# Macaron layer: the first layer's two K halves joined in PSUM, and one native group in place of two

## What is computed

```
x = x + 0.5 * ffn(layernorm(x))
x = x + mixer(layernorm(x))
x = x + 0.5 * ffn(layernorm(x))

ffn(x):   h  = layernorm(x) * gamma + beta
          w1 = (fc1_q - 128) * fc1_scales        # 256 x 1024, one scale per 128 rows and column
          y  = silu(h @ w1 + fc1_bias)
          w2 = (fc2_q - 128) * fc2_scales        # 1024 x 256, one scale per 128 rows and column
          return x + 0.5 * (y @ w2 + fc2_bias)

mixer(x): a = sigmoid(x @ Wa + ba); b = x @ Wb + bb; c = tanh(x @ Wc + bc); d = x @ Wd + bd
          s_t = a_t * s_(t-1) + (1 - a_t) * b_t
          return (c * s) @ Wy + by + d
```

## Time and profile before

| | |
|---|---|
| median of 3 runs | 780.07 us (779.71 to 782.04) |
| the profiled execution | 778.86 us, its span 777.0 us |
| TensorE busy | 736.8 us (95%) |
| ScalarE busy | 663.8 us (85%) |
| VectorE busy | 640.0 us (82%) |
| GpSimd busy | 636.8 us (82%) |
| mean granted clock | 0.985 of 2.4 GHz |

### The profile page before, as it was taken

One profiled execution on the slowest core, in us unless ns is written; L12 is line 12 of the kernel. 1 busy time (PEld: TensorE's weight loads), 2 busy tenths in 40 slices (PEclk: granted clock), 3 DMA queues, 4 the chain that ended last, 5 costly groups with the idle time before them and its releaser, 6 DMA issues.

```text
span 777.0 us, 14017 instructions
## 1 busy us (share of the span) xinstructions
PE 736.8 (95%) x3262; PEld 549.8 (71%) x3262; DVE 640.0 (82%) x1242; ACT 663.8 (85%) x1123; POOL 636.8 (82%) x821
## 2 busy tenths in 40 slices
PE   5698999999999999999999996989999999999996
PEld 4366777777777776668788783667777777777774
DVE  5377989999999998878778864779899999999886
ACT  5877999999999998778888887779989999999984
POOL 6588999999999987848666676889999999999853
PEclk7989999999999999999999999899999999999999
DMA  8640000000000000000000000000000110000001
GB/s 258 194 135 1 2 0 0 0 0 0 0 0 0 2 0 1 1 1 0 0 0 0 1 1 1 0 29 28 28 27 27 34 48 27 27 27 28 28 28 56
DMA packets 19820, 20.24 MB, mean 26 GB/s; under 512 B 1548, under 2 KB 19394, under 8 KB 19778
## 3 DMA queue, kind: packets, MB, share of 16 engines
q1 hardware_dynamic: 19680, 19.74, 7.8%
q10 hardware_dynamic: 98, 0.02, 0.0%
HBM read 11.37 MB, written 8.39 MB: 25 GB/s over the span
## 4 chain that ended last, share of the span: by engine, by line
PE 84%; issue 5%; POOL 5%; ACT 2%; DVE 2%; DMA 1%; ACTq 0%; DVEq 0%; POOLq 0%
PE ps_fc L867 28%; PE ps_z L867 26%; PE ps_z L901 13%; PE ps_fc L967 7%; PE ps_tr L860 4%; PE ps_tr L917 3%; POOL h_lo L393 2%; PE ps_fc L975 2%; POOL g_lo L403 1%; PE ps_fc L961 1%; DVE z_acc L685 1%; PE ps_z L860 1%; DMA rows<-in_L_attn_bc 1%; POOL xhat L372 1%; ACT xhat L532 0%
## 5 line engine op out<-in xcount | busy, mean ns | idle before, releaser
L685 DVE SCALAR_TENSOR_TENSOR z_acc<-ps_z,cols,z_acc 128x512 f32<-128x512 f32 x384 | 276.7, 742 | 25.2 <-PE ps_z L867 23.7
L403 POOL TENSOR_TENSOR g_lo<-g_full,g_hi 128x512 fp32r<-128x512 f32 x192 | 248.5, 1295 | 49.9 <-ACT g_hi L569 47.5
L547 ACT ACTIVATE u_sb<-ps_fc,cols 128x512 f32<-128x512 f32 x256 | 199.6, 780 | 60.8 <-PE ps_fc L867 54.9
L867 PE MATMUL ps_fc<-h_hi,q_sb 128*128 128x512 f32 x512 | 227.0, 443 | 6.1 <-DVE y_sb L674 3.9
L674 DVE SCALAR_TENSOR_TENSOR y_sb<-ps_fc,cols,u_sb 128x512 f32<-128x512 f32 x256 | 190.3, 743 | 50.5 <-ACT u_sb L547 50.4
L867 PE MATMUL ps_fc<-h_lo,q_sb 128*128 128x512 f32 x512 | 202.9, 396 | 0.0
L867 PE MATMUL ps_z<-g_hi,q_sb 128*128 128x512 f32 x384 | 155.2, 404 | 12.0 <-DVE z_acc L685 11.9
L867 PE MATMUL ps_z<-g_lo,q_sb 128*128 128x512 f32 x384 | 152.3, 397 | 0.0
L567 ACT ACTIVATE g_full<-y_sb 128x512 f32<-128x512 f32 x192 | 120.0, 625 | 9.8 <-DVE y_sb L674 9.8
L867 PEld LDWEIGHTS ps_fc<-h_hi,q_sb 128*128 128x128 f32 x512 | 97.7, 191 | 33.4 <-DVE y_sb L674 7.1
L901 PE MATMUL ps_z<-g_native,w_full 128*128 128x512 f32 x256 | 120.1, 591 | 0.0
(11 more groups left out here) (99 smaller groups left out, 980.5 us busy)
## 6 DMA issues: line engine op xcount, KB each, us to landing
resid<-in_L_attn_x SPq DMA_DIRECT2D x15, 512.0 KB, 4.4
out_x<-resid SPq DMA_DIRECT2D x15, 512.0 KB, 2.9
q_int<-in_L_ffn_fc_q SPq DMA_DIRECT2D x4, 512.0 KB, 7.0
resid<-in_L_attn_x SPq DMA_DIRECT2D x2, 256.0 KB, 3.0
out_x<-resid SPq DMA_DIRECT2D x2, 256.0 KB, 2.3
z_acc<-in_L_ffn_fc_scales SPq DMA_DIRECT2D x1, 256.0 KB, 9.2
wd_sb<-in_L_attn_Wd SPq DMA_DIRECT2D x1, 256.0 KB
wy_raw<-in_L_attn_Wy SPq DMA_DIRECT2D x2, 64.0 KB
```

The lines of the kernel that those rows point to most:

```text
L403: nc.gpsimd.tensor_tensor(g_lo[:, slot, :], g_full[:, g % 2, :], g_hi[:, slot, :].bitcast(F32), ALU.subtract).then_inc(g_ready, 1)
L547: nc.scalar.activation(u_sb[:, f % 2, :], ps_fc1[:, f % 2, 0, :], ACT.Identity, bias=col(R_B1 + f), scale=col(R_S1 + f)).then_inc(u_ready, 1)
L685: nc.vector.scalar_tensor_tensor(out=z, in0=bank_of(g, n, par), scalar=col(R_S2 + KC * g + n), in1=z, op0=ALU.mult, op1=ALU.add).then_inc( ...
L867: last = nc.tensor.matmul(out, w, v, start=start and i == 0, stop=stop and i == len(pairs) - 1)
```

## The change

The two K halves of an fc1 group now end in one PSUM bank. TensorE writes half 0 into it (half_products); ScalarE (groups 0, 1, 5, 6, 7) or VectorE (groups 2, 3, 4) scales it in place with the ratio of the two halves' scales and adds the bias over the second scale; TensorE accumulates half 1 on it (add_products, one step later, between the two chunks of fc2); silu reads the bank with the second scale. first_group, second_group, u_sb and y_sb are gone. ps_fc1 still has four banks, now one for each of four groups.

beta moves out of h: its product with the weights is computed once at the start and put into the bias (prepare_columns, beta_products, fold_beta). So h_full is gone: ScalarE rounds the turned chunk times gamma straight from PSUM (round_h), and VectorE makes h_lo from the same bank (lower_h); this VectorE step now gives turned_out. GpSimd has no h_low any more.

One group of fc2 is native (NATIVE = 1), seven are split; the native group's scale goes into first_sum. The banks of ps_z go round in order. The steps at which things are done move (the tuples below); tile 1 of a layer is normalised half by GpSimd and half by ScalarE; at the mixer's end lower_h stands before cs_full on VectorE. The warm-up products at the start are gone.

```diff
-    NATIVE = 2
+    NATIVE = 1
-    BANKS = (((1, 1, 2, 1, 0, 2, 1, 0), (0, 0, 0, 2, 1, 0, 2, 1)),
-             ((2, 2, 1, 2, 0, 1, 2, 0), (0, 0, 0, 1, 2, 0, 1, 2)))
+    BANKS = tuple(tuple((FC * KC * par + KC * g + n) % 3 for g in range(FC)) for par in range(2) for n in range(KC))
+    SCALED_ON_ACT = (0, 1, 5, 6, 7)
+    SCALED_ON_DVE = (2, 3, 4)
     STATISTICS_AT = (4, 5)
-    RESIDUAL_AT = 1
-    RSQRT_AT = (5, 3, 2)
-    NORMALISE_AT = ((6, 7), (6, 7), (5, 6))
-    TURN_AT = ((4, 5), (2, 4), (0, 2))
-    TURN_OUT_AT = ((((0, 0), 5), ((0, 1), 5), ((1, 0), 6), ((1, 1), 6)),
-                   (((0, 0), 3), ((0, 1), 4), ((1, 0), 5), ((1, 1), 5)),
-                   (((0, 0), 1), ((0, 1), 2), ((1, 0), 2), ((1, 1), 3)))
-    LOWER_PART_AT = ((4, 4), (5, 6), (3, 4))
-    WARM_UP = 14
+    VARIANCE_AT = 6
+    RESIDUAL_AT = (4, 1, 1)
+    RSQRT_AT = (5, 2, 2)
+    NORMALISE_AT = ((6, 7), (5, 6), (5, 6))
+    TURN_AT = ((3, 5), (1, 3), (0, 2))
+    TURN_OUT_AT = ((4, 6), (2, 4), (1, 3))
+    H_LOWER_AT = ((5, 7), (3, 5), (2, 4))
+    XN_LOWER_AT = (3, 5)
+    FIRST_SUM_AT = (4, 5)
     TURN_BACK_AT = (5, 6)
-    ADD_AT = (5, 6)
+    ADD_AT = (6, 7)
...
-            def affine(ln, ff, par, c, outs=(0, 1), bank=ps_tr):
...
+            def round_h(ln, ff, par, c, bank=ps_tr):
+
+                act.wait_ge(turned, 2 * ln + (c + 1))
+                wait(act, fc1_done, FC * ff - FC)
+                nc.scalar.activation(h_hi[:, par, c, :], bank[:, :], ACT.Copy,
+                                     scale=col(R_GAMMA + c)).then_inc(h_hi_ready, 1)
...
+            def scale_half(ff, f):
+
+                act.wait_ge(half_done, FC * ff + (f + 1))
+                if type(ff) is int and ff == 0 and f == 0:
+                    act.wait_ge(bias_ready, 1)
+                bank = ps_fc1[:, f % 4, :]
+                nc.scalar.activation(bank, bank, ACT.Identity, bias=bias[:, f:f + 1],
+                                     scale=ratio[:, f:f + 1]).then_inc(scaled_on_act, 1)
...
+                wait(act, g_ready, split_count(ff, g) - (0 if g == NATIVE else 1))
+                nc.scalar.activation(g_full[:, g % 2, :], bank, ACT.Silu, scale=scale)
+                wait(act, fc2_done, 2 * step - 6)
+                nc.scalar.activation(g_hi[:, g % 4, :], bank, ACT.Silu, scale=scale).then_inc(g_hi_ready, 1)
...
+            def lower_h(ln, ff, par, c, bank=ps_tr):
+
+                dve.wait_ge(h_hi_ready, 2 * ff + (c + 1))
+                nc.vector.scalar_tensor_tensor(out=h_lo[:, par, c, :], in0=bank[:, :], scalar=col(R_GAMMA + c),
+                                               in1=h_hi[:, par, c, :].bitcast(F32), op0=ALU.mult,
+                                               op1=ALU.subtract).then_inc(turned_out, 1)
...
+                        if f in SCALED_ON_DVE:
+                            scale_half(ff, f)
                         here = f >= LAG
-                        group = (ff if here else ff - 1, (f - LAG) % FC, par if here else 1 - par)
                         if before or here:
-                            add_group(*group, range(1))
-                        second_group(FC * ff + f, f)
-                        if before or here:
-                            add_group(*group, range(1, KC))
+                            add_group(ff if here else ff - 1, (f - LAG) % FC, par if here else 1 - par)
+                        if behind and f in H_LOWER_AT[before]:
+                            lower_h(ln + 1, ff + 1, 1 - par, H_LOWER_AT[before].index(f))
...
-                            if f == STATISTICS_AT[1]:
-                                variance(ln + 3)
+                        if (behind >= 3 or ff0 == 0) and f == VARIANCE_AT:
+                            variance(ln + 3)
                         if before and f in ADD_AT:
                             add_ffn(ff - 1, t - 1, ADD_AT.index(f))
...
+                for c in range(KC) if not behind else ():
+                    lower_h(2 * NT, NT, 0, c, (ps_tr, ps_tr2)[c])
                 dve.wait_ge(state_ready, t + 1)
...
-            def fc1(step, ff, f, par):
+            def half_products(ff, ln, f, par):
 
                 if f == 0:
-                    pe.wait_ge(h_ready, 2 * ff + 2)
...
+                    pe.wait_ge(turned_out, 2 * ln + 1)
...
+                wait(pe, g_hi_ready, FC * ff + (f - 3))
+                products(ps_fc1[:, f % 4, :], [(w[:, 0, f * P:(f + 1) * P], h[:, par, 0, :])
+                                               for w in q1_parts for h in (h_hi, h_lo)]).then_inc(half_done, 1)
+
+            def add_products(ff, ln, f, par):
...
+                if f in SCALED_ON_ACT:
+                    pe.wait_ge(scaled_on_act, scaled_count(ff, f, SCALED_ON_ACT))
+                else:
+                    pe.wait_ge(scaled_on_dve, scaled_count(ff, f, SCALED_ON_DVE))
+                products(ps_fc1[:, f % 4, :], [(w[:, 1, f * P:(f + 1) * P], h[:, par, 1, :])
+                                               for w in q1_parts for h in (h_hi, h_lo)],
+                         start=False).then_inc(fc1_done, 1)
...
-                        fc1(FC * ff + f, ff, f, par)
+                        half_products(ff, ln, f, par)
                         if ff0 and not before and f == LAG:
                             pe.wait_ge(mix_added, 2 * NT)
-                        if f >= LAG:
-                            fc2(ff, f - LAG, par)
+                        here = f >= LAG
+                        group = (ff if here else ff - 1, (f - LAG) % FC, par if here else 1 - par)
+                        if before or here:
+                            fc2(*group, 0)
+                        if f >= 1:
+                            add_products(ff, ln, f - 1, par)
                         elif before:
-                            fc2(ff - 1, FC + f - LAG, 1 - par)
+                            add_products(ff - 1, ln - 1, FC - 1, 1 - par)
+                        if before or here:
+                            fc2(*group, 1)
                         if (behind or ff0 == 0) and f in TURN_AT[before]:
```

More of the change, by code:

```diff
@@ L195, in macaron_kernel @@
         fc2_done = sem("fc2_done")
+        z_begun = [sem(f"z{n}_begun") for n in range(KC)]
         z_added = [sem(f"z{n}_added") for n in range(KC)]
@@ L444, in tile @@
                             rsqrt(ln0 + 1, True)
-                        for c in range(KC):
-                            if f == lower_at[c] and behind >= 1:
-                                h_low(ln + 1, ff + 1, 1 - par, c)
-                            elif f == lower_at[c] and ff0 == 0:
-                                xn_low(0, 0, c)
+                        if not before and f == 1:
+                            normalise(ln0 + 1, 1, halves[0])
+                        if ff0 == 0 and not behind and f in XN_LOWER_AT:
+                            xn_low(0, 0, XN_LOWER_AT.index(f))
+                        if behind >= 1 and f == RESIDUAL_AT[before]:
+                            residual(ln + 1, t + 1)
                         if behind >= 2 or ff0 == 0:
@@ new lines, in first_sum, with silu @@
+            def first_sum(ff, par, n):
+                act.wait_ge(fc2_done, 2 * FC * ff + (n + 1))
+                wait(act, back_done, 2 * ff - 2)
+                nc.scalar.activation(z_acc[:, par, n, :], bank_of(0, n, par), ACT.Identity,
+                                     bias=col(R_B2 + n), scale=col(R_S2 + n)).then_inc(z_begun[n], 1)
+            def silu(ff, g, par):
+                step, bank, scale = FC * ff + g, ps_fc1[:, g % 4, :], safe_scale[:, g:g + 1]
+                act.wait_ge(fc1_done, step + 1)
@@ L866, in products @@
                 for i, (w, v) in enumerate(pairs):
-                    last = nc.tensor.matmul(out, w, v, start=start and i == 0, stop=stop and i == len(pairs) - 1)
+                    last = nc.tensor.matmul(out, w, v, start=start and i == 0, stop=stop and i == len(pairs) - 1,
+                                            skip_group_check=not start)
                 return last
-            def fc1(step, ff, f, par):
+            def half_products(ff, ln, f, par):
                 if f == 0:
-                    pe.wait_ge(h_ready, 2 * ff + 2)
-                wait(pe, y_ready, step - 1)
-                for k in range(KC):
-                    if type(ff) is int and ff == 0 and f == 0:
-                        pe.wait_ge(q1_ready, k + 1)
-                    last = products(ps_fc1[:, f % 2, k, :],
-                                    [(w[:, k, f * P:(f + 1) * P], h[:, par, k, :])
-                                     for w in q1_parts for h in (h_hi, h_lo)])
-                last.then_inc(fc1_done, 1)
@@ new lines, in fc2, with beta_products @@
+                    last = nc.tensor.matmul(bank, w2_full[:, g, at], g_native[:, g, :], start=True, stop=True)
+                else:
+                    last = products(bank, [(w[:, g - NATIVE, at], v[:, g % 4, :])
```

(12 more changed lines are left out.)

297 lines of the change are left out of this document (160 added, 137 removed).

## The result

The changed kernel takes 857.25 us in the median, the kernel before 780.0 in the same rounds. One of the four executions of the changed kernel took 4159.88 us at full clock, for a reason that nothing on record shows; the others took 855.6 to 857.63, with a median of 856.87. The ratio of the mean times, taken without it, is 1.0977, with a 95% interval of 1.0949 to 1.1005: 9.8% slower. The profiled execution took 856.87 us, with a span of 855.1 and a mean granted clock of 0.997.

A forecast was written before the change was run, and what follows sets the result against it. TensorE's own work was taken as the bound. 778.86 - 24.6 (native group) - 12.4 (first tiles) + 46.5 (turn) + 56.1 (residual) + 3.3 (tile 1) = 847.8; the median being 1.2 higher, 849 us, range 800 to 880.

The forecast's parts named there:

- The three rivals: No gaps arise, 743 us, 8%; only one gap is real, 802 or 793, 7%; clock falls in gaps, 915, 7%.
- The residual's: TensorE's wait before the second turn_back for VectorE's ffn_added, tiles 1 to 15 of both layers: 56.1 us in all.
- The chain of 0.44, 0.66, 0.29, 0.69 and 0.05: Last product to VectorE's second addition, next step, variance, residual's addition, release to TensorE; less 0.235, a gap of 1.90 us.
- The turn's: TensorE's wait before xhat's second turn for VectorE's lower_h, tiles 1 to 14 of both layers: 28 x 1.66 = 46.5 us.
- ScalarE's load: ScalarE's work per tile: 13.4 us, at most 19.6 with costlier in-place scalings and silus, below the 21 us tile.
- The steady tile: Feed-forward tile after the change: 17.45 + 1.66 + 1.90 = 21.0 us against 18.22 before.
- The first tiles: First tile of each layer, its long GpSimd-caused wait gone: 6.0 us less in layer one, 6.4 in two, together 12.4.
- 1.2 net: Layer one's later start, from beta's small products, VectorE steps and tile 1's statistics: 1.2 us lost, range 0 to 4.
- The 1.7 us booked as a gain: Layer one's first tile: the slow clock, 9 products in 4 us at 0.50, would go, 1.7 us less.
- One native group: A split fc2 group replaces one native group: 0.77 us less TensorE work in each of 32 tiles, 24.6 us less.
- The clock rule: Skill's account of short pauses moving TensorE's clock up and down; the prediction had no row showing it for pauses under 2 us.
- The pace of VectorE: Back-to-back VectorE steps start 0.66 us apart at 0.742 duration; the skill's rule without its exception would add some 6 us.

The follow-up runs named there:

- e9_longer_gap: The changed kernel with the second half of the statistics moved from step 5 to 6, ahead of the residual's addition on VectorE: 918.41 us, ratio 1.1762 to the kernel before.
- e8_native2: e7_both_banks with two native fc2 groups in place of one: 764.64 us, ratio 0.9786 to the kernel before.
- e4_before_add67: The kernel before with only the residual's addition moved from steps 5 and 6 to 6 and 7: 898.13 us, ratio 1.1521.
- e7_both_banks: The changed kernel with residual's addition at steps 5, 6, h_lo heading VectorE's step, ps_z bank order shifted, GpSimd normalising a step earlier: 745.97 us, ratio 0.9552.

## Why the prediction was right

The forecast was 849.0, the range 800 to 880 and the measured median 857.25. The mechanism was as written: two places where a bank is freed by a VectorE step that stands behind an addition of TensorE's last product. The experiments removed each one alone, and both. The three rivals fall: the gaps arise; both are real; and the clock was at 1.00 in all steady tiles, though in e9_longer_gap one of the two pauses, made 0.8 us longer, brought it down. That the sum came out so close is in part luck: the steady tiles were each 0.4 us longer than forecast, about 12 us in 28 of them, and stalls of the kernel before that the forecast hadn't seen took some 8 of these back. By the terms:

*The gaps.* The residual's was put at 1.90 and was 1.88 in 15 and 1.97 in 12 of the 27 tiles with a variance; in the three without it was put at 1.61 and was 1.69. The chain of 0.44, 0.66, 0.29, 0.69 and 0.05 was right to within 0.1. The turn's was put at 1.66 and was 1.84, in eight tiles 1.92. The term that was too small is VectorE's start: I let the second addition start 0.44 behind the product, but it was still held by the in-place scaling ahead (218.00), and started 0.17 later. Over 28 places this is 5 to 6 us. The step takes 0.813, longer than the additions around it:

```profile
L563 ACT ACTIVATE ps_fc<-ps_fc,bias,ratio 128x512 f32<-128x512 f32 x160 | 121.8, 762 | 56.6 <-PE ps_fc L925 55.4
...
L582 ACT ACTIVATE g_full<-ps_fc,safe_scale 128x512 f32<-128x512 f32 x224 | 156.2, 697 | 126.7 <-PE ps_fc L925 126.2
...
L690 DVE TENSOR_SCALAR ps_fc<-ps_fc,ratio,bias 128x512 f32<-128x512 f32 x96 | 78.0, 813 | 38.5 <-PE ps_fc L925 38.5
```

These are the page's costliest groups (us busy, mean ns, idle before). ScalarE's step that writes PSUM in place takes 0.762 (0.78 was taken, between 0.39 and 1.56), and silu from PSUM 0.697, below its bound of 0.78. ScalarE's load was no issue, as said.

*The steady tile.* 21.0 was forecast; the marks 163.60 and 206.43 are two tiles apart, 21.42 each. Beside the 0.18 of the turn's gap, four transposes behind a wait cost 0.41 to the next product (210.62 to 211.03) and 0.35 without one (206.43 to 206.78), 0.12 a tile; and a product behind first_sum's bank comes 0.34 after the one before it, 0.1 more. That is 0.4.

*Missed on the other side.* The 14 tiles of a layer came only 1 to 2 us above the forecast, not 6, since the kernel before stalled in tile 2 of each layer and the change took that away. Kernel before:

```profile
62.33 0.49 PE L867 MATMUL ps_fc<-h_hi,q_sb 128*128 128x512 f32 x1 [1.36 <-DVE y_sb L674]
...
65.75 0.32 PE L860 MATMUL ps_tr<-ident,xhat 128*128 128x128 f32 x1 [1.30 <-POOL xhat L372]
```

I read the first tile and a steady one and took the tiles between for steady. Some 3 us a layer were there to be found. (Layer one's last tile had a wait of 1.03 us for ScalarE's h_hi besides, also gone.)

*The first tiles.* Of the 12.4 us only about half came. The wait of 5.4 us is gone in both layers. In layer one the start is 2.8 us later: the first DMA that TensorE waits for landed at 11.15 in place of 8.58 in this execution (8.5 to 9.6 in the seven other kernels made from the changed one), which is 2.6 of it, so that everything from there to the first fc1 product took 0.2 longer where 1.2 net was taken for the beta products. But the products were slow for longer: the first twelve, from 18.37 to 24.05, come about 0.43 apart, the pace of half clock, where in the kernel before it is the first eight. That is 0.8 us more. The windows view gives 1.00 for this stretch of the kernel after, so its mean of 0.997 leaves these products out and isn't to be compared with the 0.985 of the kernel before, whose view gives 0.50 from 9 to 19 us. Whether the removed warm-up products have a part in this no run separates. And in tile 0 the slow clock wasn't removed, only moved. Windows view after:

```profile
34.50:37.50 3.00, 3.00 (x9) 2.35 (x8) 0.96 (x2) 1.82 (x3) 2.66 (x5) 0.50 0.69 204
```

Nine products again at 0.50, as in the earlier trace rows, behind a pause of only 1.59 us in a tile that has others. The 1.7 us booked as a gain for it was no gain. In layer two the clock stayed up, and 1.9 us went to small waits in tile 0: 0.91 and 0.26 for in-place scalings, the only places where the joined halves cost something, and 0.72 for xhat. (Two small slips of the sum: nine products at 0.235 take 2.1 of the 4 us, so the slow clock was worth 1.9 and not 1.7; and 5.43 + 2.2 - 1.3 is 6.3, not 6.4.)

*One native group.* -24.6 was taken from the durations; e8_native2 says 18.7. In a steady tile it is 0.66 and not 0.77, since the split group that takes its place brings a product behind a bank's release that is 0.1 late. TensorE's busy time fell by 14.8 us, not by 25: busy time counts the overlap of products, and behind a wait a product shows longer, so it was no measure of the term.

*The clock rule.* The Trainium skill, "TensorE: Matmul & The Clock Gate", section "A second HAM failure mode: psum-queue depth-cycling", tells of a kernel in which short idle times between groups of products made the clock go up and down, at a cost in throughput. The steady tiles after don't show it with their two pauses each of 1.67 to 1.81 us; e4_before_add67 and e9_longer_gap do, with 2.39 and with 2.5 to 2.8. *The pace of VectorE.* In the earlier trace rows and in the gap above, steps start 0.66 us apart at a duration of 0.742 (218.72 and 220.04 with two additions before it), so the sum by 0.66 stood.

What stays open: why the two tiles at the ends of a layer gain less from the one native group than the steady ones (0.58 over all 32, 0.66 in the middle), and why the long pause of e4_before_add67 and e9_longer_gap brings the clock down in most tiles and in some doesn't. No run separated either.

## What to carry to other kernels

When a buffer's release moves to another engine, look at the order within that engine's step: a release that stands behind work which waits for the buffer's next writer makes a pause in every tile, though the engine has slack (VectorE was busy for 74% of the span). Put the releasing step first. Then look for the small waits that the pause had hidden, since they set the time once it is gone (here 18 us of the 111 between the changed kernel and e7_both_banks).

## What the runs showed of the hardware

Two pauses of TensorE in each steady tile, of 1.67 to 1.81 us, left the granted clock at 1.00 there. With one of them at 2.39 us and at 2.5 to 2.8 us the mean was 0.947 and 0.949. Stretches of some three microseconds at 0.50 came with 20 of 30 such pauses in the one kernel and with 25 of 27 in the other, and none with the rest, of the same length. In e9_longer_gap 23 us more of waiting cost 61 us. So here a pause in dense work had a price beyond its own length. How that price grows between 1.81 and 2.39 us no run shows. In the first tile of layer one of the kernel after it was paid behind a pause of only 1.59 us.
